# Three edits to a fused graph, attention and mixture-of-experts kernel: one array of parts with unordered scatters, weight loads side by side, and a fold on GpSimd

## What is computed

```python
x = x + relu(A_norm @ (layernorm(x) @ W.T))
h = rmsnorm(layernorm(x)); q, k, v = h@wq.T, h@wk.T, h@wv.T      # 4 heads, 2 key heads, rotary
z = layernorm(x) + softmax(mask(q k^T / sqrt(32))) v @ wo.T
flat = rmsnorm(z)
tp, ti = top_k(softmax(flat @ router_w.T), 2);  weights = tp / sum(tp)
for e in range(8):
    out += weights[:, e] * (silu(flat @ w1[e].T) * (flat @ w3[e].T)) @ w2[e].T
x = x + z + out
```

## Time and profile before

| | us |
|---|---|
| median of 3 runs | 3580.86 (3577.54 to 3583.05) |
| profiled execution | 3581.53 |
| its span, first to last instruction | 3579.8 |
| busy in the span: PE | 3099.7 (87%) |
| DVE | 2571.3 (72%) |
| POOL | 1684.5 (47%) |
| ACT | 1424.0 (40%) |

### The profile page before, as it was taken

How to read it: one execution, slowest core, us unless ns; L and a number is a source line. 1 busy time by engine, 2 the same in 40 slices (tenths; PEclk the granted TensorE clock), 3 DMA queues, 4 the chain that set the end, 5 groups by cost and what they waited for, 6 DMA issues and landing times. The chain is left out here.

```text
span 3579.8 us, 56821 instructions
## 1 busy us (share of the span) xinstructions
PE 3099.7 (87%) x22369; PEld 1361.4 (38%) x22369; DVE 2571.3 (72%) x2752; ACT 1424.0 (40%) x2843; POOL 1684.5 (47%) x1082
## 2 busy tenths in 40 slices
PE   2678889899899969999999999999999999829990
PEld 1334434344444433433333333333333333315650
DVE  8888886764554537779778877778877888227774
ACT  0000000000000004656666666666766666726660
POOL 0000000000212214666887689777789778734664
PEclk9778999999999978999999999999999999969995
DMA  9898875777768834522220000000000000012226
GB/s 379 337 385 360 360 311 241 311 300 260 269 259 328 327 131 159 209 88 85 100 70 10 10 24 18 7 13 7 11 18 18 1 12 9 13 66 59 72 66 238
DMA packets 170430, 531.94 MB, mean 149 GB/s; under 512 B 20721, under 2 KB 66938, under 8 KB 125254
## 3 DMA queue, kind: packets, MB, share of 16 engines
q1 hardware_dynamic: 124328, 473.74, 34.3%
q10 hardware_dynamic: 33024, 31.47, 2.6%
q0 software_dynamic: 12816, 23.11, 2.0%
HBM read 434.70 MB, written 92.15 MB: 147 GB/s over the span
## 5 line engine op out<-in xcount | busy, mean ns | idle before, releaser
L1231 DVE TENSOR_REDUCE unit_max<-ps_max 128x2 f32<-128x1024 f32 (+2 forms) x1088 | 1226.0, 1171 | 309.3 <-PE ps_max L1460 265.0
L1007 POOL TENSOR_TENSOR chunk_sum<-chunk_sum,probs 128x1024 f32<-128x1024 f32 x480 | 1132.1, 2359 | 309.0 <-ACT probs L1101 299.1
L1101 ACT ACTIVATE probs<-ps_ring 128x512 f32<-128x512 f32 x2112 | 1089.8, 596 | 437.3 <-PE ps_ring L1479 404.2
L566 PE MATMUL ps_gather<-ring,keep_attended 128*128 128x512 f32 x1688 | 791.6, 626 | 140.4 <-DMA ring<-in_adj 121.7
L1479 PE MATMUL ps_ring<-q_stack,keep_shared 97*128 97x512 f16 x2112 | 674.6, 385 | 28.3 <-ACT probs L1101 22.8
L1494 PE MATMUL ps_acc<-probs,keep_shared 128*32 128x256 f32 (+1 forms) x8448 | 565.3, 386 | 0.0
L566 PEld LDWEIGHTS ps_gather<-ring,keep_attended 128*128 128x128 f32 x1688 | 333.3, 202 | 542.7 <-issue 542.7
L367 DVE TENSOR_TENSOR work<-work,ring 128x2048 f32<-128x2048 f32 x195 | 446.6, 2290 | 36.0 <-DMA ring<-in_adj 32.4
L342 POOL DMA_DIRECT2D scratch_lower<-lower x13 | 7.3, 559 | 807.7 <-ACT lower L484 807.7
L1460 PE MATMUL ps_max<-k_heads,q_heads 32*128 32x512 f16 (+3 forms) x2176 | 275.6, 378 | 68.9 <-DVE unit_max L1231 47.4
L1503 PE MATMUL ps_acc<-probs,keep_ones_heads 128*32 128x256 f32 (+1 forms) x4224 | 327.3, 379 | 0.0
(11 more groups left out here) (244 smaller groups left out, 2669.2 us busy)
## 6 DMA issues: line engine op xcount, KB each, us to landing
ring<-in_adj SPq DMA_DIRECT2D x302, 1024.0 KB, 14.1
keep_shared<-in_adj SPq DMA_DIRECT2D x45, 1024.0 KB, 11.1
scratch_slots<-empty_rows SPq DMA_DIRECT2D x16, 2080.0 KB, 14.1
scratch_parts<-empty_part SPq DMA_DIRECT2D x8, 2048.0 KB, 13.3
moe_parts<-scratch_parts SPq DMA_DIRECT2D x64, 256.0 KB, 4.4
moe_x_rows<-scratch_slots SPq DMA_DIRECT2D x39, 260.0 KB, 2.7
x_in<-in_x SPq DMA_DIRECT2D x16, 256.0 KB, 13.4
x_in<-in_x ACTq DMA_DIRECT2D x16, 256.0 KB, 8.0
```

The lines of the kernel that those rows point to most:

```text
L566: last = nc.tensor.matmul(bank[:], support[:, s * SUB + c, :], tile_of[g, is_again][:, c * BT:(c + 1) * BT], start=(first and c == 0), sto ...
L1007: steps.then(nc.gpsimd.tensor_tensor(totals, totals, weights, ALU.add))
L1101: nc.scalar.activation(probs[:, q % SLOTS, i, kv, :, lo:], halves(bank)[:, :, lo:], ACT.Exp, scale=SCALE).then_inc(ring_read, 1)
L1231: nc.vector.tensor_reduce(unit_max[:, half % 2, heads, s % 2, unit], ps_max[:, base:base + HEADS, at:at + width], AX_X, ALU.max).then_inc( ...
```

## The change

In `attention_stage`, POOL adds the two sums of a half into one when the half closes, and `combine` multiplies that one sum. The transfers that cleared `parts0` and `parts1`, their tile `empty_part` and its memset go. In `expert_stage` there is one array `parts`. Every row of it that is read is written by exactly one scatter. Scatters wait for no other scatter: the last block's eight, and each group's four, which signal by the group's buffer. The three weight transfers are issued at once, each with its own semaphore. DVE makes the table of groups first and the remainders of the weights later, the third after the first group's tokens. The closing loop loads two pieces a block and adds once.

```diff
-        adds += 1 if together(q) else 3 if q in opens_half else 2
+        adds += (1 if together(q) else 3 if q in opens_half else 2) + (q in closes_half)
-    FILLS = {1: 2, 2: 3, 3: 4, 4: 4, 5: 4, 6: 3, 7: 3, 8: 2}
+    FILLS = {1: 2, 2: 3, 3: 4, 4: 4, 5: 4}
-        empty_part = sb("empty_part", [P, SUB * C])
@@ fill_next
-                else:
-                    chain, at = divmod(n - SLOT_FILLS - 1, PART_FILLS)
-                    sp.dma_start(dram[f"parts{chain}"][at * FILLED:(at + 1) * FILLED, :].rearrange(
-                        "(p r s) c -> p r (s c)", r=FILL_ROWS, s=SUB),
-                        empty_part[:].unsqueeze(1).to_broadcast([P, FILL_ROWS, SUB * C])).then_inc(parts_emptied, 16)
@@ add_pair
+                if q in closes_half:
+                    steps.then(nc.gpsimd.tensor_tensor(totals[:, 0], totals[:, 0], totals[:, 1], ALU.add))
...
-            nc.gpsimd.memset(empty_part[:], 0.0).then_inc(tables_set, 1)
@@ combine
-                for i in range(2):
-                    for r in range(NREP):
-                        last = nc.tensor.matmul(out[r * HD:(r + 1) * HD, 0:HALF], keep["ones_heads"][:],
-                                                chunk_sum[:, half % 2, i, r], start=False, stop=True,
-                                                skip_group_check=True)
+                for r in range(NREP):
+                    last = nc.tensor.matmul(out[r * HD:(r + 1) * HD, 0:HALF], keep["ones_heads"][:],
+                                            chunk_sum[:, half % 2, 0, r], start=False, stop=True,
+                                            skip_group_check=True)
...
-    CHAINS = 2
+    BUFFERS = 2
-        parts = sb("parts", [P, PB, CHAINS, TOPK, BT])
+        parts = sb("parts", [P, PB, TOPK, BT])
...
             for n, name in enumerate(WEIGHTS):
-                if n:
-                    sp.wait_ge(weights_in, 16 * n)
-                sp.dma_start(exact[name][:], dram[name]).then_inc(weights_in, 16)
+                sp.dma_start(exact[name][:], dram[name]).then_inc(weights_in[n], 16)
...
-                for c in range(CHAINS):
-                    for k in range(TOPK):
-                        at = (k * NB + T) * BT
-                        sp.dma_start(parts[:, n, c, k, :], dram[f"parts{c}"][at:at + BT, :].rearrange(
-                            "(p s) c -> p (s c)", s=SUB)).then_inc(parts_loaded[n], 16)
+                for k in range(TOPK):
+                    at = (k * NB + T) * BT
+                    sp.dma_start(parts[:, n, k, :], dram["parts"][at:at + BT, :].rearrange(
+                        "(p s) c -> p (s c)", s=SUB)).then_inc(parts_loaded[n], 16)
...
             for n in range(SUB * TOPK):
                 s, k = n // TOPK, n % TOPK
-                if n:
-                    pool.wait_ge(last_scattered, 16 * n)
...
                 for s in range(SUB):
-                    earlier = g * (SUB // CHAINS) + s // CHAINS
-                    if earlier:
-                        pool.wait_ge(y_scattered[s % CHAINS], 16 * earlier)
                     pool.indirect_dma_start(
-                        dram[f"parts{s % CHAINS}"], bass.IndirectOffsetOnAxis(y_index[:, g % 2, s:s + 1], 0),
-                        y_rows[:, g % 2, s, :], None, bounds_check=TOPK * N - 1, oob_is_err=False
-                    ).then_inc(y_scattered[s % CHAINS], 16)
+                        dram["parts"], bass.IndirectOffsetOnAxis(y_index[:, g % BUFFERS, s:s + 1], 0),
+                        y_rows[:, g % BUFFERS, s, :], None, bounds_check=TOPK * N - 1, oob_is_err=False
+                    ).then_inc(y_scattered[g % BUFFERS], 16)
@@ expert_stage, DVE, head of the stream
-            for n, name in enumerate(WEIGHTS):
-                dve.wait_ge(weight_hi_ready, n + 1)
-                nc.vector.scalar_tensor_tensor(out=w_lo[name][:], in0=exact[name][:], scalar=WEIGHT_SCALE,
@@ expert_stage, DVE, behind the table
+            split_weight(0)
+            split_weight(1)
             split_tokens_low(0)
+            split_weight(2)
@@ scale_parts
                 if g >= 2:
-                    for c in range(CHAINS):
-                        dve.wait_ge(y_scattered[c], 16 * (SUB // CHAINS) * (g - 1))
+                    dve.wait_ge(y_scattered[g % BUFFERS], 16 * SUB * (g // BUFFERS))
...
-                nc.vector.tensor_tensor(parts[:, n, 0], parts[:, n, 0], parts[:, n, 1], ALU.add).then_inc(chain_step, 1)
-                dve.wait_ge(chain_step, T + 1)
-                nc.vector.tensor_tensor(parts[:, n, 0, 0, :], parts[:, n, 0, 0, :], parts[:, n, 0, 1, :], ALU.add
+                nc.vector.tensor_tensor(parts[:, n, 0, :], parts[:, n, 0, :], parts[:, n, 1, :], ALU.add
@@ down
+                if k == 0:
+                    pe.wait_ge(weight_lo_ready, len(WEIGHTS))
...
-            pe.wait_ge(weight_lo_ready, len(WEIGHTS))
             pe.wait_ge(table_ready, 2)
             turn_tokens(0)
+            pe.wait_ge(weight_lo_ready, 2)
```

More of the change, by code:

```diff
@@ L938, in fill_next @@
                 if n == 0:
-                    sp.wait_ge(tables_set, 3)
+                    sp.wait_ge(tables_set, 2)
                 if n < SLOT_FILLS:
@@ L1410, in _ @@
                 find_shift(half)
-            dve.wait_ge(tables_set, 10)
+            dve.wait_ge(tables_set, 9)
             for q in range(PAIRS):
@@ L1580, in _ @@
             pe.wait_ge(constants_set, 3)
-            pe.wait_ge(tables_set, 10)
+            pe.wait_ge(tables_set, 9)
             pe.wait_ge(small_in, 16 * len(SMALL))
@@ L1672, in expert_stage @@
         small_in = sem("small_in")
-        weights_in = sem("weights_in")
+        weights_in = [sem(f"weights_in{n}") for n in range(3)]
         ln2_ready = sem("ln2_ready")
@@ L1693, in expert_stage @@
         y_scaled = sem("y_scaled")
-        y_scattered = [sem(f"y_scattered{n}") for n in range(CHAINS)]
+        y_scattered = [sem(f"y_scattered{n}") for n in range(BUFFERS)]
         parts_loaded = [sem(f"parts_loaded{n}") for n in range(PB)]
-        chain_step = sem("chain_step")
         parts_added = sem("parts_added")
@@ L1721, in _ @@
                              ).then_inc(x_loaded[g % XB], 16)
-            for c in range(CHAINS):
-                sp.wait_ge(y_scattered[c], 16 * (SUB // CHAINS) * GROUPS)
+            for n in range(BUFFERS):
+                sp.wait_ge(y_scattered[n], 16 * SUB * len(range(n, GROUPS, BUFFERS)))
             for T in range(NB):
@@ L1758, in _ @@
                 for s in range(SUB):
-                    earlier = g * (SUB // CHAINS) + s // CHAINS
-                    if earlier:
-                        pool.wait_ge(y_scattered[s % CHAINS], 16 * earlier)
                     pool.indirect_dma_start(
-                        dram[f"parts{s % CHAINS}"], bass.IndirectOffsetOnAxis(y_index[:, g % 2, s:s + 1], 0),
-                        y_rows[:, g % 2, s, :], None, bounds_check=TOPK * N - 1, oob_is_err=False
-                    ).then_inc(y_scattered[s % CHAINS], 16)
+                        dram["parts"], bass.IndirectOffsetOnAxis(y_index[:, g % BUFFERS, s:s + 1], 0),
+                        y_rows[:, g % BUFFERS, s, :], None, bounds_check=TOPK * N - 1, oob_is_err=False
+                    ).then_inc(y_scattered[g % BUFFERS], 16)
             for T in range(NB):
                 pool.wait_ge(parts_added, T + 1)
-                result = parts[:, T % PB, 0, 0, :]
+                result = parts[:, T % PB, 0, :]
                 nc.gpsimd.tensor_tensor(result, result, residual[:, T * BT:(T + 1) * BT], ALU.add).then_inc(result_ready, 1)
@@ L1817, in _ @@
                 act.wait_ge(result_ready, T + 1)
-                act.dma_start(dram["out"].rearrange("(b s p) c -> b p s c", s=SUB, p=P)[T], split(parts[:, T % PB, 0, 0, :])
+                act.dma_start(dram["out"].rearrange("(b s p) c -> b p s c", s=SUB, p=P)[T], split(parts[:, T % PB, 0, :])
                               ).then_inc(result_stored[T % PB], 16)
@@ L1855, in _, with split_weight @@
             nc.vector.tensor_copy(expert_index[:], expert_of[:]).then_inc(table_ready, 1)
+            def split_weight(n):
+                name = WEIGHTS[n]
+                dve.wait_ge(weight_hi_ready, n + 1)
+                nc.vector.scalar_tensor_tensor(out=w_lo[name][:], in0=exact[name][:], scalar=WEIGHT_SCALE,
+                                               in1=w_hi[name][:], op0=ALU.mult, op1=ALU.subtract
+                                               ).then_inc(weight_lo_ready, 1)
             def split_tokens_low(g):
@@ L1985, in program @@
                             ("lower", (NB, P, BT), F32), ("q_hi", (P, N), F16), ("q_lo", (P, N), F16), ("k_hi", (P, N), F16),
-                            ("slots", (NE * N + GROUP, ROW), F32), ("parts0", (TOPK * N, C), F32),
-                            ("parts1", (TOPK * N, C), F32)):
+                            ("slots", (NE * N + GROUP, ROW), F32), ("parts", (TOPK * N, C), F32)):
```

15 lines of the change are left out of this document (5 added, 10 removed).

## The result

The change makes the kernel 1.6% faster: 3523.91 us median of four runs (3518.88 to 3529.45), against 3579.32 us for four runs of the kernel before (3577.54 to 3583.05). The ratio is 0.9844, interval 0.9827 to 0.9861. That is 55.4 us less; the forecast was 3527, 53.7 less. One of nine executions of the kernel before on the chip of the last three experiments took 4132.49 us at a granted clock of 0.73, where all others had 0.94, and is left out of every comparison.

The account below looks back on a forecast made before the run. Bounds by stage: TensorE in attention and experts, a chain in the transition, DMA engines in the closing stretch. Terms summed to -53.7 us from 3581.5, 3527.8; 3527 predicted after a 0.6 us median offset, range 3507 to 3547.

Parts of the forecast that it names:

- Combine, -10.7: Attention: four of eight combine passes go, 0.43 us each, 13.3 us over 31 combines, a fifth absorbed: minus 10.7 us.
- Fold, +4, bounds 0 and 43: Attention: 32 more GpSimd adds of 1.35 us, mostly hidden: plus 4 us; all 43 if the cover were gone.
- rival that GpSimd becomes the bound (3555): Attention: three quarters of the folds' 43 us show instead of 4, giving 3555 us; chance 0.1.
- End of attention, +0.4: Before the last combine: the fold adds 1.35 us, half of the passes takes off 0.96: plus 0.4 us.
- Clearing, -1: Attention: eight 2 MB fills and a memset go, easing only shift-row waits: minus 1 us, bounds 0 and minus 3.
- Transition, -19: Attention to experts: scatter and third-array legs meet near 3202, first product 19 us earlier; bounds 15 and 22.
- Experts and drain, -6.4: Unordered scatters: 2 us in the expert stage, 4.4 in the drain at 1.28 us spacing; bounds 2 and 9.
- rival of scatters that don't overlap (3792): Expert stage: scatters into one array each wait for the one before, 265 us more, 3792 us; chance 0.03.
- Closing sums, -21: Closing stretch: 8.4 MB fewer loads at the running 394 GB/s save 21 us.
- the second rival: Closing stretch held by its buffers' turn, minus 13, and third array no sooner, minus 15: 3539 us; chance 0.15.
- rival of more than I count (3511): Shorter combines fully paid, fold free, transition gives 22 and closing stretch 27: 3511 us; chance 0.1.

Follow-up runs that it names:

- the last three experiments: Kernel before with only fold and shorter combine; changed kernel with third weight array in two transfers; the latter plus eight closing buffers: attention 1780.8 us, transition 23.4, total 3506.36.
- fold_undone: Changed kernel without the GpSimd fold, combine multiplying both sums again: attention 1796.8 us, 10.5 more than after; end of routing 29.8 us against 30.3.
- rows_ordered: Changed kernel with the last block's eight scatters each waiting for the one before: 38.7 us from last slot index to first expert product, 25.3 after.
- fold_twice: Changed kernel with a second, useless GpSimd add of the same size behind each fold: attention 1781.7 us; end of routing 31.7 us against 30.3.
- only_fold: Kernel before with the fold and shorter combine alone: attention 1780.8 us, 16.4 less than before; closing stretch 71.0 us.

## Why the prediction held, step by step

- **Combine, -10.7.** The price of one was right, 0.43 us, in all the halves that repeat. Whether a fifth is absorbed in the others, as I let it, stays open. With a fold, ten traces took 1778.7 to 1786.9 us for attention, mean 1783.1; without it, before and fold_undone, 1797.2 and 1796.8. The difference of the means is 13.9 us, near the 31 x 0.43 = 13.3 that would need no absorption; the trace after, at -11.0, is what a fifth of absorption would leave. Two traces without a fold against a spread of 8 us cannot decide it. I did not settle where the spread comes from. It lies in the halves that do not repeat; some of them have routing (the first half of block 5 took 41.06 us before, 42.55 with fold_undone, 42.22 after, 39.01 with rows_ordered), others come ahead of any routing (the first half of block 1: 14.65, 15.75, 14.21 and 16.20).
- **Fold, +4, bounds 0 and 43.** Its cover holds; where halves repeat, it costs nothing, and neither does a second one. The rival that GpSimd becomes the bound (3555) has fallen. By the Trainium skill (SBUF — State Buffer, "Who interferes with whom") each fold that meets routing would hold VectorE; up to 10 us were worked out from that, with eight such folds. The trace agrees with the hold, 1.10 us for a step of 0.19, but only three folds held a step, 2.5 us of VectorE's time in all. The scatter's issue of 2.69 us beside VectorE's 3.00 us shows the same the other way round: it ends 0.84 us after VectorE does, and the one of 3.95 us before ended 0.85 us after the earlier trace rows.
- **End of attention, +0.4.** Measured +0.5; fold_undone gives it back, fold_twice adds 1.35.
- **Clearing, -1.** Nothing that a run shows, which was the lower bound.
- **Transition, -19.** Measured -19.3, and by the mechanism named: two legs that meet. Inside, sizes were off by up to 1.3 us in pairs that cancelled, which is luck. The trace's DMA packets, the third array's being told by their 12288 bytes, give the weights' leg: the first two arrays were across 9.7 us after the first issue, forecast 10.7, and the third 9.1 us later, forecast 8.3 (its own packets moved at 146 GB/s, not 168): 18.8, forecast 19.0. The last scatter stood 1.7 us in its issue, not 3, and landed 8.05 us after that issue began, 6.3 without the stall and not 5.75: from the first issue to the last landing 17.2 us, forecast 14.7 to 17.8. The first product came 6.6 us behind that landing, forecast 6.7. Two of the forecast's own sums are 0.2 to 0.3 us too long (3196.3 + 2.76 is 3199.1; 3200.9 + 2.76 + 1.7 is 3205.4); nothing hangs on that.
- **Experts and drain, -6.4.** Measured -7.6: 1.6 between the first and the last expert product, forecast 2, and 6.0 behind the last, forecast 4.4. The rival of scatters that don't overlap (3792) has fallen: with a landing of 2.12 us they are 1.29 us apart. That the pace holds with more than two in flight is shown by the transition alone, where the eight are 1.31 us apart and a scatter beside the weights takes 6.5 us to land (rows_ordered), which makes some five in flight, an estimate. PE's wait for `y_rows` fell from 7.8 us to 1.5, and the closing loads begin 15.0 us after the last expert product (3458.3 to 3473.3), forecast less than 18.
- **Closing sums, -21.** This term was mis-sized: -17.4 between the two traces. The step that failed is the rate: 8.4 MB were taken off at the running 394 GB/s as though the rest would still move at it. With half the bytes in a turn the four buffers bound, and the stretch ran at a mean of 256 GB/s. That is the mechanism of the second rival, whose figure of -13 was too low, while its other half, a third array no sooner than today, did not occur. Before took 66.7 us for it here and 71.0 in only_fold, the nine traces with one array and four buffers 48.9 to 52.1, so the two traces do not settle the term to better than some 4 us; the eight buffers' 39.8 lies outside all of these, and is 26.9 below 66.7, close to the 26.8 that 8.4 MB make at the stretch's mean of 313.

The sum of -53.7 stands against -57.3 between the two traces: attention gave 3.3 us more than counted, the experts 1.2, the untouched graph stage 2.6, and the closing sums 3.6 less. So the forecast came as near as it did partly because misses had opposite signs, and the 2.6 and the 3.3 are no larger than what these stretches vary by from trace to trace. The rival of more than I count (3511) is near what after took with eight buffers (3511.64), not what the change gave.

## What to carry to other kernels

When a loop of load, add and store is cut to fewer bytes, price it twice: the bytes at the running rate, and one turn of a buffer times the number of turns. Here the second ruled, and the freed memory, spent on more buffers, gave another 10 us. When several legs of a start-up run beside each other, undoing them one by one gives prices that add up to more than the whole (33 against 19.3), and speeding one of them up alone gives little (1.9 us for a transfer that lands 3.5 us sooner). And extra work for an engine that is busy three quarters of the time cost nothing that could be seen where its reader came three pairs later, and its full 1.35 us at the one place where the reader waits.

## What was not expected of the hardware

- The array of 114 rows is loaded by few DMA engines. In the window 3175:3180, when the first two arrays have landed and the last scatters still move, the share is 0.41 of 16 engines and the rate 172 GB/s, and of that array's packets six are in flight at a time for 7.3 of their 9.6 us. In two pieces, 112 rows and 2, up to some sixteen are in flight, the packets take 6.1 us, and the array was rounded 3.5 us sooner. The Trainium skill (DMA: Bandwidth & Descriptors, "How many engines (k)") lets the number of engines be the largest up to 16 that divides the rows: 6 for 114, 16 for 112. The trace agrees: six packets in flight, and sixteen.
- Scatters issued beside the weights land late: 6.5 us after the issue for the first in rows_ordered, and 8.05 for the last of the eight after, of which 1.7 are the stall of its issue, against 2.29 once the weights are gone.
- Unordered scatters are issued every 1.29 us, 0.98 for the instruction and 0.30 between two: 10 spacings in a row in the drain with two in flight, and 1.31 in the transition with some five.
- The same attention code takes 1778.7 to 1786.9 us from one trace to another. Half of its halves repeat to 0.03 us; all of the spread lies in the others, with routing and without.
